# A cross-attention and expert kernel: the order of its first stage, of its loads, and an early table load

## The reference

```python
x = x + _L0_xattn_ref(_layernorm(x), ctx_4096, ctx_4096)
#   qh = softmax(qh, axis=3)               over the 8 columns of a head
#   kh = softmax(kh, axis=1)               over the 512 columns of the context row
#   kvs = einsum('bnhd,bnhe->bhde', kh, vh)
#   out = einsum('bnhd,bhde->bnhe', qh, kvs)
x = x + _L0_ffn_ref(_layernorm(x), U1, V1, U2, V2, b1, b2)
x = x + _L1_xattn_ref(_layernorm(x), ctx_4096, Wq, Wk, Wv, Wo)
x = x + _L1_ffn_ref(_layernorm(x), gate_w, bias, Wg, Wu, Wd, Sg, Su, Sd)
```

## Time and profile before

| | |
|---|---|
| three runs | 763.07, 765.58, 766.16 us |
| median | 765.58 us |
| profiled execution | 762.17 us, span 760.3 us |
| busy in the span | PE 701.6 us (92%), PEld 411.0, DVE 324.7, ACT 217.7, POOL 186.7 |
| chain that ended last | PE 75%, DMA 8%, DVE 7%, issue 4%, ACT 2% |
| mean granted clock | 0.984 |

### The profile page before, as it was taken

The page is one execution under the profiler, slowest core; times in us unless marked ns, Lnnn a source line. Parts: engine busy times, 40 slices in busy tenths (PEclk is TensorE's granted clock), DMA queues, the critical chain, the costliest instruction groups (busy, mean ns, idle before and its releaser), DMA issues.

```text
span 760.3 us, 9543 instructions
## 1 busy us (share of the span) xinstructions
PE 701.6 (92%) x2560; PEld 411.0 (54%) x2561; DVE 324.7 (43%) x808; ACT 217.7 (29%) x595; POOL 186.7 (25%) x265
## 2 busy tenths in 40 slices
PE   5998899989999899999999979987998999899992
PEld 3554443435678776777776645443444444445440
DVE  3786633531014665667667475484111112112211
ACT  3453332314224333333242332321221212122210
POOL 1234310100000000022020222222344554355541
PEclk9999999999999999999999989999999999999997
DMA  9700400022000000000040000027767447655533
GB/s 335 290 1 1 165 1 1 0 81 85 1 1 0 1 1 15 0 15 2 15 93 6 14 15 16 14 66 274 223 163 175 88 84 226 173 97 86 107 56 41
DMA packets 20434, 57.55 MB, mean 76 GB/s; under 512 B 3584, under 2 KB 6912, under 8 KB 18720
## 3 DMA queue, kind: packets, MB, share of 16 engines
q0 software_dynamic: 9136, 19.04, 13.6%
q1 hardware_dynamic: 9200, 34.15, 12.5%
q10 hardware_dynamic: 2064, 3.93, 1.4%
HBM read 42.93 MB, written 14.32 MB: 75 GB/s over the span
## 4 chain that ended last, share of the span: by engine, by line
PE 75%; DMA 8%; DVE 7%; issue 4%; ACT 2%; POOLq 1%; POOL 1%; ACTq 0%; DVEq 0%
PE ps L1076 42%; PE ps L1231 11%; PE ps L1067 5%; DMA out<-rq,sidx 3%; PE ps L1219 3%; DMA rq<-z_rows,gidx 3%; PE ps L1203 3%; PE ps L1152 2%; PE ps L1153 2%; PE ps L1162 2%; DVE rq L894 1%; DMA r<-in_ctxT 1%; ACT r L661 1%; PE ps L1099 1%; PE ps L1100 1%
## 5 line engine op out<-in xcount | busy, mean ns | idle before, releaser
L1076 PE MATMUL ps<-kv,rq 128*128 x432 | 192.9, 596 | 0.5 <-ACT rq L718 0.5
L1076 PEld LDWEIGHTS ps<-kv,rq 128*128 128x128 f32 x432 | 79.6, 191 | 87.4 <-issue 87.2
L1076 PE MATMUL ps<-zT,r 128*128 128x256 f32 (+1 forms) x400 | 92.8, 388 | 0.6 <-ACT rq L652 0.6
L1231 PE MATMUL ps<-r 128*128 128x512 f32 x192 | 86.2, 599 | 0.0
L1076 PEld LDWEIGHTS ps<-zT,r 128*128 128x128 f32 x400 | 75.0, 190 | 14.9 <-issue 4.3
L661 ACT ACTIVATE r<-ps,snm 128x128 f32<-128x128 f32 x128 | 45.4, 367 | 106.8 <-DVE snm L947 106.8
L1026 DVE TENSOR_TENSOR rq<-ps,rq 128x256 f32<-128x256 f32 x36 | 15.3, 425 | 140.5 <-ACT rq L722 140.5
L541 POOL DMA_INDIRECT out<-rq,sidx x36 | 57.4, 1596 | 67.8 <-DMA out<-rq,sidx 44.4
L494 POOL DMA_INDIRECT slots<-tokw,sloti x32 | 32.3, 1010 | 140.9 <-DVE sloti L1006 133.5
L469 POOL TENSOR_SCALAR ve<-mv 128x1 f32<-128x1 f32 x32 | 7.2, 226 | 235.3 <-DVE mv L863 235.2
L1231 PEld LDWEIGHTS ps<-r 128*128 128x128 f32 x192 | 35.9, 193 | 39.8 <-issue 39.8
(11 more groups left out here) (177 smaller groups left out, 942.2 us busy)
## 6 DMA issues: line engine op xcount, KB each, us to landing
kv<-in_experts SPq DMA_DIRECT2D x9, 1536.0 KB, 8.0
r<-in_Wq SPq DMA_DIRECT2D x1, 3072.0 KB, 10.2
r<-in_Wo SPq DMA_DIRECT2D x1, 3072.0 KB, 11.5
r<-in_ctx SPq DMA_DIRECT2D x8, 256.0 KB, 9.1
xr<-in_x SPq DMA_DIRECT2D x8, 256.0 KB, 8.9
z_rows<-zrow SPq DMA_DIRECT2D x8, 256.0 KB, 2.9
r<-in_shared SPq DMA_DIRECT2D x1, 1536.0 KB, 11.2
r<-in_V SPq DMA_DIRECT2D x1, 1376.0 KB, 11.1
```

The costliest lines, as they stand in the source:

```text
L1076: mm = pe.matmul(out, lhs(k), rhs(k), start=(k == 0), stop=(k == n - 1))
L1231: mm = pe.matmul(ps[:, 7, :], oT[:, j % 2, m, :], wo[:, m, :], start=(m == 0), stop=(m == NQT - 1))
```

## The change

Three edits.

1. The list of the first stage is laid out anew. A head does the first tiles: statistics 0 and 1, `a_prep 0`, `a_t 0`, `a_q 0`, `a_prep 1`, unit 0, `a_stat 2`, `a_kvs 0`, `a_t 1`, `a_prep 2`, `a_q 1`, unit 1, `a_stat 3`. Then a loop over the tile j of `a_out`: `a_out` and `x1` of j, `a_kvs` of j+1, `a_t` and `a_q` of j+2, a unit, `ln_z` of j-2, `ln_stat` of j-1, `a_stat` of j+4, `a_prep` of j+3, `ln_t` of j-3, and a second unit for j = 1, 3, 5, 6. So `a_kvs` of the next tile stands right behind `a_out`, and the transposition of a normalised row one step later than before. `f_in` comes behind the last unit and `ln_t 4`; `ln_t 5` behind `f_in`, as before.
2. ACT's four loads are issued as `ctxT` first piece, `wv`, `ctxT` second piece, `wk`.
3. ACT then waits for the first memsets and does one exponential of 4 zeros a partition, whose result is overwritten later.

No instruction of the stage is removed; one is added.

```diff
-        prog += [("a_stat", 0), ("a_stat", 1)]
-
-        per_step = (1, 2, 1, 2, 2, 2, 1, 2, 1, 0)
-        prog.append(("a_prep", 0))
-        for s in range(J + 2):
-            if s < J:
-                prog.append(("a_t", s))
-            if 2 <= s:
-                prog.append(("a_out", s - 2))
-                prog.append(("x1", s - 2))
-            if s == J + 1:
-                prog.append(("f_in", 0))
-            if s + 1 < J:
-                prog.append(("a_prep", s + 1))
-            if 1 <= s <= J:
-                prog.append(("a_q", s - 1))
-            if per_step[s]:
-                prog.append(("kv", fill.pop(0)))
-            if 1 <= s <= J:
-                prog.append(("a_kvs", s - 1))
-            if 4 <= s:
-                prog.append(("ln_z", 1, s - 4))
-            if s + 2 < J:
-                prog.append(("a_stat", s + 2))
-            if 3 <= s:
-                prog.append(("ln_stat", 1, s - 3))
-            if per_step[s] > 1:
-                prog.append(("kv", fill.pop(0)))
-            if 4 <= s:
-                prog.append(("ln_t", 1, s - 4))
+        def unit():
+            return ("kv", fill.pop(0))
+
+        prog += [("a_stat", 0), ("a_stat", 1), ("a_prep", 0), ("a_t", 0), ("a_q", 0), ("a_prep", 1), unit(), ("a_stat", 2),
+                 ("a_kvs", 0), ("a_t", 1), ("a_prep", 2), ("a_q", 1), unit(), ("a_stat", 3)]
+        for j in range(J):
+            prog += [("a_out", j), ("x1", j)]
+            if j + 1 < J:
+                prog.append(("a_kvs", j + 1))
+            if j + 2 < J:
+                prog += [("a_t", j + 2), ("a_q", j + 2)]
+            prog.append(unit())
+            if j >= 2:
+                prog.append(("ln_z", 1, j - 2))
+            if j >= 1:
+                prog.append(("ln_stat", 1, j - 1))
+            if j + 4 < J:
+                prog.append(("a_stat", j + 4))
+            if j + 3 < J:
+                prog.append(("a_prep", j + 3))
+            if j >= 3:
+                prog.append(("ln_t", 1, j - 3))
+            if j in (1, 3, 5, 6):
+                prog.append(unit())
+        prog += [("f_in", 0), ("ln_t", 1, J - 3)]
...
-            act.dma_start(wv, wv_d.rearrange("p (k m) -> p k m", k=KC)).then_inc(s_wv, 16)
             for h in range(2):
                 act.dma_start(ctxT[:, :, h * 256:(h + 1) * 256], ctxT_d[:, :, h * 256:(h + 1) * 256]).then_inc(s_ct[h], 16)
                 if h == 0:
-                    act.dma_start(wk, wk_d.rearrange("p (k m) -> p k m", k=KC)).then_inc(s_wk, 16)
+                    act.dma_start(wv, wv_d.rearrange("p (k m) -> p k m", k=KC)).then_inc(s_wv, 16)
+            act.dma_start(wk, wk_d.rearrange("p (k m) -> p k m", k=KC)).then_inc(s_wk, 16)
+            act.wait_ge(s_ms, 2)
+            act.activation(ssum[:, 0, :], zero[:, 0:4], ACT.Exp)
```

## The result

The changed kernel's median is 760.64 us over 20 executions, that of the kernel before 765.25 us over 20. The ratio is 0.9937, with a 95% interval of 0.9913 to 0.9961: 4.8 us less, between 3.0 and 6.7. The forecast was 760.7. Two executions of the kernel before, taken beside e5 to e8, lasted 1926 and 4236 us and are in none of the ratios.

A forecast was written before the change was run, and what follows sets the result against it. PE's first stage, with 5.80 us of waits and a low clock behind one, was taken to bound; first `f_gu` moves from 91.36 to 86.5, gain 4.9 us off the 765.58 median: 760.7, forecast's own range 759 to 762.5, whole range 756.5 to 764.7.

The forecast's parts named there:

- The order: First stage on PE: the new list removes the `ln_z` waits; unit 0 ends at 14.1, first `f_gu` at 86.5 us.
- the waits at `a_out 1`, `a_out 5`, `f_in` and `f_gu`: PE, first stage: remaining or new waits of 1.0 and 0.8 (DVE chain), 0.95 (unit 13's copy) and 0.4 us.
- The 0.4 us that the method was short: Same addition tried on the old order gave first `f_gu` at 91.0 against 91.36; 0.4 was added to the new sum.
- The start: Loads ahead of unit 0: later of ctxT and Wv in at 10.0 us (bounds 9.0, 12.0); unit 0 lasts 4.1.
- my own signs of being wrong: Unit 0 starting behind 11 us or lasting 5, DVE chain above 4.7, clock 0.50 before `f_gu`, or span no shorter.
- The clock: PE behind the old 2.33 us `ln_z` wait: granted clock 0.50 loses 1.7 us, which the new order saves.
- The table load at nothing: ACT's 1.28 us table load moved ahead: first `a_t` 1.28 us earlier, worth nothing because unit 0 waits for loads.
- A: Smaller gain: Wv in at 12.0, unit 0 lasting 5.2; gain 1.8 us, time 763.8; chance 0.20.
- B: Larger gain: PE waits of 1.0, 0.8 and 0.95 us don't appear; gain 7.6, time 758.0; chance 0.09.
- C: Gain given back in a later stage set by something that doesn't move; no change, 765.6 us; chance 0.10.
- D: Slower: four short PE waits each lower the clock, costing 1.7 us each; loss 1.9, time 767.5; chance 0.05.
- E: Load order and table load alone are worth nothing; counted inside the forecast, no chance of its own.

The follow-up runs named there:

- e5: Changed kernel with the next tile's `a_kvs` moved back behind each step's unit; ratio to before 0.9954 (0.9925 to 0.9983), 10 executions.
- e8: Changed kernel with `f_in` in PSUM bank 3 and Silu's table loaded early on ACT; 759.01 us, ratio to before 0.9916 (0.9886 to 0.9946).
- e6: Changed kernel with the reciprocal over half the columns (results wrong, only first stage read); first `f_gu` at 83.86 us, stage 1.71 us shorter.
- e7: Changed kernel with the first `f_in` written to PSUM bank 3 instead of 7; first `f_gu` at 83.76 us, stage 1.16 us shorter.
- e1: Kernel before with only ACT's four loads reordered; ratio 0.9971 (0.9938 to 1.0003) over 10 executions, first `f_gu` at 89.23 us.
- e2: Kernel before with only the small exponential that loads ACT's table early; first `f_gu` at 91.00 us, no ratio given.
- e10: Kernel before, unchanged, profiled a second time; first `f_gu` at 91.86 us, 77.08 behind unit 0's end.
- e9: Changed kernel without the early table load; first `f_gu` at 85.91 us, 71.92 behind unit 0's end.
- e3: Kernel before with only the first stage's new order, old loads, no early table; ratio 0.9965 (0.9935 to 0.9995) over 12 executions.
- e11: Changed kernel, unchanged, profiled a second time; first `f_gu` at 84.75 us, 71.92 behind unit 0's end.
- e4: Changed kernel with normalised rows transposed in their old step (j-2), not one later; ratio 1.0022 (0.9995 to 1.0050), first `f_gu` at 93.96 us.

## Why the prediction was right

*The order, forecast to about half a microsecond.* I had unit 0's end at 14.1 and `f_gu` at 86.5, 72.4 us apart; it is 71.93. Of the steps, the waits at `a_out 1`, `a_out 5`, `f_in` and `f_gu` were to be 1.0, 0.8, 0.95 and 0.4, start to start, and are 0.88, 0.48, 1.08 (79.72 to 80.80) and 0.39 (84.75 to 85.14). The one at `a_out 3`, 0.1, is 0.04. The two on the DVE chain are smaller, because the chain is 4.8 us seen from PE (`a_out 0` ends at 17.13 + 1.72 = 18.85, `a_out 1` starts at 23.64) and not 4.9, and at `a_out 5` because DVE was through with the statistics of step 4 a little sooner: its reciprocal starts at 50.88, 0.24 behind `a_out 4`'s end, where I had 0.5. The new wait ahead of `f_in`, which nothing in the trace of before showed and only the code gives away, was the most useful term: without it the stage would have been put 1.1 us too short.

*The 0.4 us that the method was short.* e6 and e7 explain it. Each wait costs 0.26 more than its idle time. I had added 0.1 for each of four; the missing 0.16 for each make 0.6, of which I had found 0.4 short.

*The start, mis-sized.* This is the step that failed, a term of the sum: when the later of ctxT's first piece and Wv would be in. "The two hold the same bytes in any order, so I take 10.0 for the later one", with 9.0 as the lower end. In the nine profiles with the new loads unit 0 started between 7.85 and 9.25, in the four with the old ones between 10.07 and 10.48. The first context row landed 2.5 to 2.9 us behind its issue in the new order, 4.9 to 5.2 in the old one. Same bytes does not mean same time. The 4.1 us that I kept for unit 0 were those of one profile, the shortest of all 13; it lasted 4.8 us in the mean of the nine and 4.7 in the mean of the four. The profiled execution of the changed kernel has 5.25, one of my own signs of being wrong. From the means of unit 0's end, 14.95 for the four and 13.26 for the nine, the loads are worth 1.7 us and not 0.2.

*The clock, counted as certain.* The 1.7 us behind the long wait were in my sum in full. They are there in both profiles of the kernel before and in neither of e1 and e2, so they may be worth 0.8 in the mean or the full 1.7; that is open. e1 and e2 also lose some 1.4 us to the low clock later, at the end of the feed-forward (last section), where before and e10 lose none; no profile of the 13 has both losses, so a part of what is saved here may be paid there. With 0.8 the parts are 3.5 for the order, 1.7 for the start and 0.8 for the clock, 6.0 in all, where I had 4.9 (3.0, 0.2 and 1.7). With the full 1.7 they make 6.8 (from 3.46, 1.69 and 1.69). The measured 4.8 has 4.9 and 6.0 inside its interval, and 6.8 just outside.

*Luck in the number.* That 760.7 lies within 0.1 us of the measured 760.64 is luck. The interval of the gain is nearly 2 us wide to either side, and the stage gained 6.2 us in the first pair of profiles and 7.1 in the second (91.86 to 84.75), and not 4.9. The mechanism was right: the waits that vanish, the waits that come, and the size of the order's part to 0.5 us.

*The table load at nothing.* e2 and e9 agree, each with one execution. The Trainium skill (ScalarE: Activation LUTs, What ACT_TABLE_LOAD costs) states 2.66 us for a load with its drain, so an estimate by it has `a_t 0` 2.66 us sooner. In e9 and the changed kernel, which differ in it alone, `a_t 0` moved from 6.76 to 5.82, by 0.94, and in e2 against before from 8.94 to 7.91, by 1.03. Counted from DVE's reading of the first context row, which came at other times, e2 gained the whole 1.28 of the load (1.93 us, before 3.21) and the changed kernel 1.05 (2.16, in e9 3.21). There ACT was still busy with the early load and the small exponential until its first real one at 4.88. The drain isn't seen.

*The rivals.* A, the late start, failed in its first half (Wv landed earlier, not later) and came true in its second: unit 0 lasted 5.1 us in e2 and up to 5.25 with the new loads, near its bound of 5.2. The Trainium skill (TensorE: Matmul & The Clock Gate, The HAM clock gate) was cited for a low clock as the default, which activity releases. The slow matmuls of unit 0 in every profile fit that, but the granted clock reads 1.00 there, so that it is the clock is argued from the durations and not shown. That the isolated `a_t 0` is the reason isn't shown, since e3 and e10 have no such gap and took 4.9 and 4.7. B fails: all three waits that it left out appear, start to start 0.88, 0.48 and 1.08. C fails, as the later stages start earlier by what the first gains (4.7 us at 244, where one drop of the clock has cost 1.5). D fails: in none of the profiles of the changed kernel, e3, e5 to e9 and e11 is the granted clock below 1.00 before `f_gu`. Waits of under 1 us can stand ahead of a low clock elsewhere, though; see below. E is wrong in its premise: the order of the loads is worth 1.7 us, and only the table load brought nothing that could be seen.

## What to carry to other kernels

When a fast engine waits for a slow one's result in a hand-written order, look for the one consumer that stands a place too early. Moving it one step back was worth 9.3 us in the new order (e4 undoes it), up to 1.7 of it by the clock. The rest of the new order brought nothing without it. Forecast a stage by adding start-to-start times of the engine that sets it, step by step, with each slower chain beside it, and read in the code every wait that a moved step will meet, above all a PSUM bank that has to be copied out. Take the start of a kernel, and the clock behind a wait, from several profiles, and look at the mean granted clock before you explain why one execution is longer than another.

## What the runs showed of the hardware

- The order of loads in one queue changes when a load of another queue lands. With ctxT (4 x 128 pieces of 1 KB) ahead of Wv (128 pieces of 6 KB) on ACT's queue, the first context row on SP's queue landed at 3.7 us instead of 5.7. The Trainium skill (DMA: Bandwidth & Descriptors, Queues, rings and completion order) has each DMA engine take turns between queues by packets. That fits small pieces letting the other queue through sooner, but the load that goes first is also the smaller one (512 KB against 768 KB), and no run here varied either alone. So the cause is argued and not shown.
- The clock behind a wait is not settled by the wait's length. Behind the same 2.33 us it fell to 0.50 in two profiles of four (both of the kernel before). And behind the same pair of waits of 0.76 and 0.68 us at the end of the feed-forward, in the same order in every kernel, it fell in 5 of 13 profiles. Of the two profiles of the changed kernel one is among them and the other (e11) isn't, so there it differs from execution to execution. The changed kernel's timeline and window there:

```profile
154.03 1.13 PE L1160 MATMUL ps<-rq,r 96*128 96x512 f32 x2 [0.76 <-DVE rq L923]
155.83 5.40 PE L1170 MATMUL ps<-r,rq 128*128 128x512 f32 x8 [0.68 <-ACT rq L646]
```

```profile
157.00:158.00 1.00, 1.00 (x3) 0.34 (x1) 0.69 (x1) 0.00 (x0) 0.00 (x0) 0.50 0.00 0
```

  The eight matmuls of L1170 take 5.40 us here; in the profile of before they take 4.03 behind the same two waits, at a clock of 1.00:

```profile
161.94 4.03 PE L1172 MATMUL ps<-r,rq 128*128 128x512 f32 x8 [0.68 <-ACT rq L648]
```

- A wait of PE costs about 0.26 us beyond its idle time (0.24 where e7 takes one away): 0.16 by which the last matmul before it is drawn longer than its spacing, and 0.10 by which the first one behind it is slower.
